# Attention scores by row tiles: one head to 64 rows of the array, keys' low part out of PSUM

## The chip, the cores and the metric

The kernel runs on one core of a Trainium2 chip. The metric is the device time of one execution in microseconds (us). The core's engines run side by side and meet at semaphores: TensorE (PE) multiplies, VectorE (DVE) and ScalarE (ACT) work element by element and are the ones that empty PSUM here, GpSimd (POOL) does arithmetic in SBUF, and SyncE (SP) issues nearly all DMAs.

## The reference, cut to what matters

There are 128 graphs of 128 nodes with 512 features, and one adjacency mask for all. Two layers of attention with 8 heads of 64 follow each other.

```python
def layer0(x, adj, Wq, bq, Wk, bk, Wv, bv, Wo, bo):
    q, k, v = x @ Wq + bq, x @ Wk + bk, x @ Wv + bv        # each split into 8 heads of 64
    scores = einsum('bqhd,bkhd->bhqk', q, k) / sqrt(64) + (1 - adj) * -1e9
    return einsum('bhqk,bkhd->bqhd', softmax(scores), v) @ Wo + bo

x = layernorm(x + layer0(x, adj, ...))
x = layernorm(x + layer1(x, adj, ...))      # the same without Wo and bo
```

## The kernel before, in words

**Tiles.** Two graphs make a group of 256 tokens (`GB = 2`, `T = 256`), 64 groups in all. Products are made in fp32r, a four-byte format of lower precision, and so each operand is split into a high part in fp32r and the low part that is left, and a product is three matmuls: high by high, high by low, low by high. Weights are split once. Queries and keys come out of the projection with features on partitions: tile c of four holds heads 2c (rows 0 to 63) and 2c+1 (rows 64 to 127).

**Scores.** A score matmul needs one head's 64 rows alone. Before, the keys are kept in blocks with zeros: `k_hi[:, b, c]` is 128 x 256, where columns 0 to 127 hold the even head in the upper 64 rows and zeros below, and columns 128 to 255 the odd head in the lower rows and zeros above. One matmul of 128 rows and 256 columns then gives both heads' scores. There are four score banks in PSUM, two to a graph (`ps_score[b][i]`, four heads each).

**Making q and k.** A projection unit (`unit(l, g, u, group, i)`) fills one of two banks, `ps_proj[u % 2]`. Units i = 0, 1 are q, 2 and 3 are k (24 matmuls of 256 columns each), 4 and 5 are v (12 of 512). ScalarE empties q into `q_hi`, VectorE then subtracts (`q_low`, line 848). For k, ScalarE writes the sum with its bias to `k_raw` (line 635), and the bank is free. VectorE casts the two halves of rows into their blocks (line 858) and makes the odd head's low part (line 860), GpSimd makes the even head's (line 1132).

**Order.** Every engine's order is written by hand, as phases A and B of a loop over groups. Phase A of turn g works on scores and softmax of layer 1 of group g-2 and on the projections of layer 0 of group g; phase B on scores of layer 0 of group g and projections of layer 1 of group g-1. On TensorE phase A is: scores, `wo` of the group before, units 0 to 3, attend of graph 0, units 4 and 5, attend of graph 1. Phase B is: scores, units 6 to 10 (i = 0 to 4), attend of graph 0, unit 11 (i = 5), `wo`, attend of graph 1. `need_bank` makes a unit wait until the bank's last user has emptied it; who that is, `emptied` says:

```python
if i < 4:
    return (q_lo_set if i < 2 else k_raw_set)[l], group * 2 + i % 2 + 1
return v_set[l], group * 2 + i - 3
```

**Softmax.** VectorE adds the mask and takes the maximum out of the score banks (line 833), ScalarE takes exponentials (647), VectorE inverts the sums (841), GpSimd scales (1126), VectorE transposes blocks of 32 (893), and DMAs carry them into `prob_t` (302), which attend (451) reads. After attend of layer 0, ScalarE copies to `at_hi` (727), VectorE makes `at_lo` (935) for `wo`; VectorE adds residuals (931, 943), takes statistics (867), GpSimd makes `rstd` (1120) and VectorE normalises (883). GpSimd also adds a bias to a copy of x1 (1138).

Of the kernel before, what the change touches and what calls it, by code (L numbers as in the profile page):

```python
# [16 lines left out]
HALVES = H // HB  # L38
# [17 lines left out]
def adj_resnorm_kernel(nc, x_tok, x_feat, adj, wts, biases, out):  # L56
# [6 lines left out]
    with ExitStack() as ctx:  # L63
# [16 lines left out]
        q_hi, q_lo = sb("q_hi", [P, NC, T], F32R), sb("q_lo", [P, NC, T], F32R)  # L80
        k_hi, k_lo = (sb(n, [P, GB, NC, 2, NODES], F32R) for n in ("k_hi", "k_lo"))
        k_raw = sb("k_raw", [P, 2, T])
# [63 lines left out]
        zeros_set = sem("zeros_set")  # L146
# [9 lines left out]
        k_raw_set = [sem(f"k_raw_set{l}") for l in range(2)]  # L156
        k_hi_set = [sem(f"k_hi_set{l}") for l in range(2)]
        k_lo_even_set = [sem(f"k_lo_even_set{l}") for l in range(2)]
        k_lo_odd_set = [sem(f"k_lo_odd_set{l}") for l in range(2)]
# [68 lines left out]

        def k_block(part, i, e):

            return part[e * HD:(e + 1) * HD, :, 2 * i:2 * i + 2, e, :]

        def k_source(e):
            return k_raw[e * HD:(e + 1) * HD].rearrange("p c (b n) -> p b c n", b=GB)
# [162 lines left out]
        def _(pe):  # L397
# [30 lines left out]
            def scores(l, group, b, banks_free, count):  # L428

                pe.wait_ge(q_lo_set[l], group * 2 + 2)  # L430
                pe.wait_ge(k_lo_even_set[l], group * 2 + 2)
                pe.wait_ge(k_lo_odd_set[l], group * 2 + 2)
                tok = slice(b * NODES, (b + 1) * NODES)
                for i in range(HALVES):

                    need(pe, banks_free, count + 2 * b + i + 1)
                    for c in (2 * i, 2 * i + 1):
                        ps_pair = ps_score[b][i][:, 2 * (c % 2):2 * (c % 2) + 2, :]
                        parts = [(q_hi, k_hi), (q_hi, k_lo), (q_lo, k_hi)]
                        for n, (qp, kp) in enumerate(parts):  # L440
                            last = pe.matmul(ps_pair, qp[:, c, tok], kp[:, b, c], start=(n == 0), stop=(n == 2))  # L441
                    last.then_inc(score_done[l], 1)

            def attend(l, group, b):
# [140 lines left out]
        def _(act):  # L585
# [191 lines left out]
        def _(dve):  # L777
# [167 lines left out]
            def phase_a(g):  # L945
# [40 lines left out]
                if live(g):  # L986
                    k_split(0, g, 0)
# [259 lines left out]
```

## Time and profile before

| | |
|---|---|
| median of three runs | 3415.47 us (3413.94 to 3415.5) |
| span of the profiled execution | 3412.5 us |
| PE busy | 3262.3 us, 96% of the span |
| DVE busy | 2875.9 us, 84% |
| ACT busy | 1697.6 us, 50% |
| POOL busy | 1558.5 us, 46% |
| granted clock of TensorE, mean | 0.991 |

The median lies 3.0 us over the span that the profile covers. Busy time of PE is that of matmuls in a pipeline, so that it covers small waits too; the distance from one matmul's start to the next (its pitch) tells more than its duration.

### The profile page before, as it was taken

Reading aid. Unit: us, or ns where it says so; the run is one execution under the profiler, and the core shown is the slowest. Engines: PE = TensorE matmul, PEld = TensorE weight load, DVE = VectorE, ACT = ScalarE, POOL = GpSimd, SP = SyncE. Lnnn points to the kernel's source line nnn. Section 1 sums busy time; section 2 is a strip of 40 time slices with the busy share of each in tenths; the row PEclk is TensorE's granted clock in tenths of the full one; section 3 lists DMA queues with packets and bytes.
Section 4 is the critical chain, followed back from the end, with each engine's and each line's share of the span. In section 5 each row is a group of like instructions: output and inputs, shape, how many; then the busy total and the mean of one; then the engine's idle time right before and its main releaser. Section 6 shows DMA issues by size and latency. Waiting matters only on the chain.

```text
span 3412.5 us, 78555 instructions
## 1 busy us (share of the span) xinstructions
PE 3262.3 (96%) x24076; PEld 2921.1 (86%) x24076; DVE 2875.9 (84%) x8342; ACT 1697.6 (50%) x5777; POOL 1558.5 (46%) x1350
## 2 busy tenths in 40 slices
PE   6999999999999999999999999999999999999995
PEld 5888888888888888888888888888888888888884
DVE  6888888888888888888888888888888888888885
ACT  4554454455445544544554555455445545554552
POOL 2444444444444444444444444444444444444442
PEclk8999999999999999999999999999999999999997
DMA  4233333333333333333333333333333333333332
GB/s 141 75 95 93 86 90 95 92 86 90 93 92 85 95 94 85 92 92 92 86 91 95 90 83 95 95 84 95 90 92 86 92 95 89 84 95 95 85 93 65
DMA packets 346122, 310.46 MB, mean 91 GB/s; under 512 B 38896, under 2 KB 301296, under 8 KB 346096
## 3 DMA queue, kind: packets, MB, share of 16 engines
q1 hardware_dynamic: 344800, 309.48, 35.0%
q10 hardware_dynamic: 1296, 0.67, 0.1%
q8 instruction: 12, 0.20, 0.0%
q14 instruction: 14, 0.11, 0.0%
HBM read 75.11 MB, written 33.55 MB: 32 GB/s over the span
## 4 chain that ended last, share of the span: by engine, by line
PE 37%; issue 22%; DVE 22%; DMA 5%; POOL 5%; SPq 3%; ACT 3%; DVEq 1%; POOLq 0%; ACTq 0%
PE ps_proj L405 28%; PE ps_score L441 6%; DMA prob_t<-blocks_t 5%; DVE prob L833 4%; DVE k_hi L858 3%; SPq L302 3%; DVE xt_hi L795 3%; ACT k_raw L635 3%; DVE blocks_t L893 2%; PE ps_att L451 2%; DVE x_res L943 2%; POOL k_lo L1132 2%; POOL prob L1126 2%; DVE x L883 2%; PE ps_proj L414 1%
## 5 line engine op out<-in xcount | busy, mean ns | idle before, releaser
L647 ACT ACTIVATE prob<-prob,neg_max 128x128 f32<-128x128 f32 x2048 | 792.6, 390 | 341.5 <-DVE neg_max L833 341.4
L1126 POOL TENSOR_TENSOR prob<-prob,inv_sum 128x512 f32<-128x512 f32 x512 | 523.1, 1043 | 867.1 <-DVE inv_sum L841 867.1
L1132 POOL TENSOR_TENSOR k_lo<-k_raw,k_hi 64x512 fp32r<-64x512 f32 x256 | 388.4, 1517 | 664.9 <-DVE k_hi L858 664.9
L405 PE MATMUL ps_proj<-xt_hi,w_hi_q 128*128 128x256 f32 x2048 | 593.3, 290 | 36.0 <-ACT xt_hi L657 13.5
L405 PE MATMUL ps_proj<-xt_lo,w_hi_q 128*128 128x256 f32 x2048 | 581.4, 284 | 0.0
L405 PE MATMUL ps_proj<-xt_hi,w_lo_q 128*128 128x256 f32 x2048 | 581.2, 284 | 0.0
L405 PE MATMUL ps_proj<-xt_hi,w_hi_k 128*128 128x256 f32 x2048 | 579.8, 283 | 0.8 <-DVE q_lo L848 0.8
L405 PE MATMUL ps_proj<-xt_lo,w_hi_k 128*128 128x256 f32 x2048 | 579.6, 283 | 0.0
L405 PE MATMUL ps_proj<-xt_hi,w_lo_k 128*128 128x256 f32 x2048 | 579.3, 283 | 0.0
L860 DVE TENSOR_TENSOR k_lo<-k_raw,k_hi 64x512 fp32r<-64x512 f32 x256 | 571.2, 2231 | 8.8
L833 DVE CUSTOM_DVE_ANT_0 prob<-ps_score,mask 128x128 f32<-128x128 f32 x2048 | 462.0, 284 | 4.8 <-issue 0.7
L405 PEld LDWEIGHTS ps_proj<-xt_hi,w_hi_q 128*128 128x128 f32 x2048 | 394.3, 193 | 63.5 <-issue 25.4
L635 ACT ACTIVATE k_raw<-ps_proj,bk_col 128x256 f32<-128x256 f32 x512 | 312.8, 719 | 244.2 <-PE ps_proj L405 140.6
L893 DVE STREAM_TRANSPOSE blocks_t<-prob 128x512 f32<-128x512 f32 x512 | 340.7, 694 | 97.9 <-POOL prob L1126 88.3
L414 PE MATMUL ps_proj<-w_hi_v,xt_hi 128*128 128x512 f32 x1024 | 415.0, 405 | 0.3 <-ACT k_raw L635 0.3
L414 PE MATMUL ps_proj<-w_lo_v,xt_hi 128*128 128x512 f32 x1024 | 402.0, 393 | 0.0
L414 PE MATMUL ps_proj<-w_hi_v,xt_lo 128*128 128x512 f32 x1024 | 398.5, 389 | 0.0
L405 PEld LDWEIGHTS ps_proj<-xt_lo,w_hi_q 128*128 128x128 f32 x2048 | 394.9, 193 | 0.1
L405 PEld LDWEIGHTS ps_proj<-xt_hi,w_lo_q 128*128 128x128 f32 x2048 | 394.7, 193 | 0.0
L405 PEld LDWEIGHTS ps_proj<-xt_hi,w_hi_k 128*128 128x128 f32 x2048 | 393.2, 192 | 1.2 <-DVE q_lo L848 1.0
L405 PEld LDWEIGHTS ps_proj<-xt_lo,w_hi_k 128*128 128x128 f32 x2048 | 393.2, 192 | 0.0
L405 PEld LDWEIGHTS ps_proj<-xt_hi,w_lo_k 128*128 128x128 f32 x2048 | 393.2, 192 | 0.0
(89 smaller groups left out, 6928.3 us busy)
## 6 DMA issues: line engine op xcount, KB each, us to landing
prob_t<-blocks_t SPq DMA_DIRECT2D x1024, 128.0 KB, 2.7
y<-x_feat SPq DMA_DIRECT2D x128, 256.0 KB, 2.7
x_res<-x_tok SPq DMA_DIRECT2D x64, 512.0 KB, 3.4
prob_t<-prob SPq DMA_DIRECT2D x512, 64.0 KB, 2.1
out<-y SPq DMA_DIRECT2D x128, 256.0 KB, 2.7
prob_t<-blocks_t SPq DMA_DIRECT2D x256, 64.0 KB, 2.1
y<-y SPq DMA_DIRECT2D x256, 64.0 KB, 2.1
prob<-w_q SPq DMA_DIRECT2D x2, 512.0 KB, 5.8
```

The lines of the kernel that those rows point to most:

```text
L302: sp.dma_start(prob_t[b][:, n].rearrange("p e c q -> p (e c q)"), blocks_t[n * SQ:(n + 1) * SQ].rearrange("p n e c q -> p n (e c q)")).the ...
L405: last = pe.matmul(ps_out[:, i * T:(i + 1) * T], wp[:, c, cols], xp[:, c, :], start=(c == 0 and n == 0), stop=(c == NC - 1 and n == 2))
L414: last = pe.matmul(ps_out[:, :], xp, wp[:, c, :], start=(c == 0 and n == 0), stop=(c == NC - 1 and n == 2))
L441: last = pe.matmul(ps_pair, qp[:, c, tok], kp[:, b, c], start=(n == 0), stop=(n == 2))
L635: last = act.activation(dst, src, ACT.Identity, bias=bias[:, m:m + 1])
L647: last = act.activation(prob[b][:, i, n, :], prob[b][:, i, n, :], ACT.Exp, bias=neg_max[l][b][:, i, n:n + 1], scale=-1.0, accum_out=row_su ...
L795: dve.tensor_copy(x0_half(xt_hi[0], half), x0_half(xt_raw, half)).then_inc(x0_hi_set, 1)
L833: last = dve.tensor_tensor_reduce(prob[b][:, i, n, :], ps_score[b][i][:, n, :], mask[l][:], -SCALE, BIG, ALU.add, ALU.min, neg_max[l][b][: ...
L860: dve.tensor_tensor(k_block(k_lo, i, 1), raw, hi.bitcast(F32), ALU.subtract).then_inc(k_lo_odd_set[l], 1)
L893: dve.transpose(blocks_t[:, :, i].rearrange("p n h q -> p h n q"), prob[b][:, i].rearrange("p h (n k) -> p h n k", k=SQ)).then_inc(blocks_ ...
L1126: pool.tensor_tensor(prob[b][:, i], prob[b][:, i], inv_sum[l][b][:, i, :].unsqueeze(2).to_broadcast([P, HB, NODES]), ALU.mult).then_inc(no ...
L1132: pool.tensor_tensor(k_block(k_lo, i, 0), k_source(0), k_block(k_hi, i, 0).bitcast(F32), ALU.subtract).then_inc(k_lo_even_set[l], 1)
```

## The change

The score matmuls take one head each: 64 rows, the even head on the upper row tile of the array, the odd one on the lower, 128 columns, in turn, and each into a bank of its own (`ps_score[b][e]` now holds the four even or the four odd heads). The keys lose their zero blocks and have the layout of the queries. ScalarE writes `k_hi` straight from the bank, VectorE makes `k_lo` from the bank and `k_hi` as it does for q, in four instructions a unit, with a stride of 32 elements in SBUF. `k_raw`, its casts, GpSimd's share and the clearing of the blocks at the start are gone. Both score banks of a graph are awaited before its first score matmul. A bank of k counts as emptied once `k_lo` is written.

```diff
-        k_hi, k_lo = (sb(n, [P, GB, NC, 2, NODES], F32R) for n in ("k_hi", "k_lo"))
-        k_raw = sb("k_raw", [P, 2, T])
+        k_hi, k_lo = (sb(n, [P, NC, T], F32R) for n in ("k_hi", "k_lo"))
...
-                    return (q_lo_set if i < 2 else k_raw_set)[l], group * 2 + i % 2 + 1
+                    return (q_lo_set if i < 2 else k_lo_set)[l], group * 2 + i % 2 + 1
...
-                for i in range(HALVES):
-
-                    need(pe, banks_free, count + 2 * b + i + 1)
-                    for c in (2 * i, 2 * i + 1):
-                        ps_pair = ps_score[b][i][:, 2 * (c % 2):2 * (c % 2) + 2, :]
-                        parts = [(q_hi, k_hi), (q_hi, k_lo), (q_lo, k_hi)]
-                        for n, (qp, kp) in enumerate(parts):
-                            last = pe.matmul(ps_pair, qp[:, c, tok], kp[:, b, c], start=(n == 0), stop=(n == 2))
-                    last.then_inc(score_done[l], 1)
+                need(pe, banks_free, count + 2 * b + 2)
+                parts = [(q_hi, k_hi), (q_hi, k_lo), (q_lo, k_hi)]
+                for c in range(NC):
+                    for n, (qp, kp) in enumerate(parts):
+                        for e in range(HALVES):
+                            rows = slice(e * HD, (e + 1) * HD)
+                            last = pe.matmul(ps_score[b][e][:, c, :], qp[rows, c, tok], kp[rows, c, tok],
+                                             start=(n == 0), stop=(n == 2))
+                            if c == NC - 1 and n == 2:
+                                last.then_inc(score_done[l], 1)
...
-                        dst = k_raw[:, n, :].rearrange("p (b j n) -> p b n j", b=GB, n=SQ)
+                        dst = k_hi[:, m, :].rearrange("p (b j n) -> p b n j", b=GB, n=SQ)
...
-                for e in range(2):
-                    hi, raw = k_block(k_hi, i, e), k_source(e)
-                    dve.tensor_copy(hi, raw).then_inc(k_hi_set[l], 1)
-                dve.wait_ge(k_hi_set[l], group * 4 + 2 * i + 2)
-                dve.tensor_tensor(k_block(k_lo, i, 1), raw, hi.bitcast(F32), ALU.subtract).then_inc(k_lo_odd_set[l], 1)
+                    for b in range(GB):
+                        tok = slice(b * NODES, (b + 1) * NODES)
+                        hi, lo = (t[:, m, tok].rearrange("p (j n) -> p n j", n=SQ) for t in (k_hi, k_lo))
+                        last = dve.scalar_tensor_tensor(lo, src[:, tok].rearrange("p (n j) -> p n j", j=BLK),
+                                                        bk_col[l][:, m:m + 1], hi.bitcast(F32),
+                                                        ALU.add, ALU.subtract)
+                last.then_inc((q_lo_set if i < 2 else k_lo_set)[l], 1)
...
-                if live(m):
-                    k_low_even(1, m, 1)
                     copy_x1(m, 0)
                     copy_x1(m, 1)
```

TensorE's order around the attend of graph 0 in phase B of turn 2, before; `ps_proj1` is the bank of the second v unit, `w_hi_v1` the weights of layer 1's v:

```order
L414 MATMUL ps_proj0<-w_hi_v1,xt_lo1 128x512
L451 MATMUL ps_att<-prob_t0,v_first 64x128 [waits v_set0,probt_in0,at1_set]
L451 MATMUL ps_att<-prob_t0,v_first 64x128 x7
L414 MATMUL ps_proj1<-w_hi_v1,xt_hi1 128x512 [waits k_raw_set1]
L414 MATMUL ps_proj1<-w_lo_v1,xt_hi1 128x512
```

And the same place now:

```order
L382 MATMUL ps_proj0<-w_hi_v1,xt_lo1 128x512
L419 MATMUL ps_att<-prob_t0,v_first 64x128 [waits v_set0,probt_in0,at1_set]
L419 MATMUL ps_att<-prob_t0,v_first 64x128 x7
L382 MATMUL ps_proj1<-w_hi_v1,xt_hi1 128x512 [waits k_lo_set1]
L382 MATMUL ps_proj1<-w_lo_v1,xt_hi1 128x512
```

The order is the same; the unit's first matmul now waits for the semaphore of VectorE's `k_lo` instead of that of ScalarE's copy.

VectorE's order in the same phase B from the last transposes to the residual, before (`rstd1` and `y` belong to layer 1's layernorm, `at_lo` to the attend of layer 0):

```order
L893 STREAM_TRANSPOSE blocks_t<-prob1 128x4x4x32 [waits norm_set0]
L931 TENSOR_TENSOR y<-prob_t1,x1_res 128x4x4x32 [waits x1_lo_set,y_out1,x1t_in1,x1_res_set,x0_lo_set,at1_in1]
L867 BN_STATS stats1<-y 128x6 [waits sum_set1]
L870 BN_AGGR mean_var1<-stats1 128x2 [waits stats_set1]
L872 TENSOR_SCALAR var_eps1<-mean_var1 128x1 [waits mean_set1]
L935 TENSOR_TENSOR at_lo<-ps_att,at_hi 128x512 [waits at_hi_set]
L883 TENSOR_SCALAR y<-y,mean_var1,rstd1 128x512 [waits rstd_set1]
L858 CAST k_hi<-k_raw 64x2x2x128 [waits k_raw_set1]
L858 CAST k_hi<-k_raw 64x2x2x128
L860 TENSOR_TENSOR k_lo<-k_raw,k_hi 64x2x2x128 [waits k_hi_set1]
L943 TENSOR_TENSOR x_res<-ps_proj0,x_res 128x512 [waits x_res_set,wo_done]
```

And now:

```order
L841 STREAM_TRANSPOSE blocks_t<-prob1 128x4x4x32 [waits norm_set0]
L879 TENSOR_TENSOR y<-prob_t1,x1_res 128x4x4x32 [waits x1_lo_set,y_out1,x1t_in1,x1_res_set,x0_lo_set,at1_in1]
L815 BN_STATS stats1<-y 128x6 [waits sum_set1]
L818 BN_AGGR mean_var1<-stats1 128x2 [waits stats_set1]
L820 TENSOR_SCALAR var_eps1<-mean_var1 128x1 [waits mean_set1]
L883 TENSOR_TENSOR at_lo<-ps_att,at_hi 128x512 [waits at_hi_set]
L831 TENSOR_SCALAR y<-y,mean_var1,rstd1 128x512 [waits rstd_set1]
L805 SCALAR_TENSOR_TENSOR k_lo<-ps_proj1,bk_col1,k_hi 128x32x4 [waits k_hi_set1]
L805 SCALAR_TENSOR_TENSOR k_lo<-ps_proj1,bk_col1,k_hi 128x32x4 x3
L891 TENSOR_TENSOR x_res<-ps_proj0,x_res 128x512 [waits x_res_set,wo_done]
```

The place of k's work is unchanged, behind `at_lo` and the normalise of `y`; four instructions stand for three. (In this unrolled turn there is no group whose x0 is cast between them; in the loop `x0_high` stands ahead of the residual.)

GpSimd in phase B, before:

```order
L1120 TENSOR_TENSOR rstd1<-var_eps1,minus_half 128x1 [waits ln_set1,eps_set1]
L1131 REGISTER_ALU
L1132 TENSOR_TENSOR k_lo<-k_raw,k_hi 64x2x2x128 [waits k_hi_set1]
L1136 REGISTER_ALU
L191 REGISTER_ALU [waits ln_set0]
L1138 TENSOR_TENSOR x1_res<-x1,bv1_row 128x512 [waits sum_set1]
L1138 TENSOR_TENSOR x1_res<-x1,bv1_row 128x512 [waits sum_set1,ln_set0]
```

And now:

```order
L1066 TENSOR_TENSOR rstd1<-var_eps1,minus_half 128x1 [waits ln_set1,eps_set1]
L1077 REGISTER_ALU
L166 REGISTER_ALU [waits ln_set0]
L1079 TENSOR_TENSOR x1_res<-x1,bv1_row 128x512 [waits sum_set1]
L1079 TENSOR_TENSOR x1_res<-x1,bv1_row 128x512 [waits sum_set1,ln_set0]
```

The two copies of x1 have moved up: nothing that waits for keys stands between them and `rstd` now.

## Rows read from the trace of the kernel before

**Rows 1.** The page: span and busy times.
```profile
span 3412.5 us, 78555 instructions
PE 3262.3 (96%) x24076; PEld 2921.1 (86%) x24076; DVE 2875.9 (84%) x8342; ACT 1697.6 (50%) x5777; POOL 1558.5 (46%) x1350
```

**Rows 2.** Windows: one turn of the loop; stretch, length, busy times, clock, DMA.
```profile
1696.87:1748.91 52.04, 50.74 (x378) 45.44 (x377) 44.43 (x131) 26.26 (x90) 24.31 (x21) 1.00 0.35 91
```

**Rows 3.** Waits of the whole run: total us, times, longest.
```profile
PE ps_att L451 <- DMA prob_t<-blocks_t: 66.6, 62, 1.2
PE ps_proj L405 <- DVE x_res L943: 11.6, 61, 0.2
```

**Rows 4.** Timeline, end of phase A: start, length, engine, line, operation, idle before.
```profile
1741.16 0.60 ACT L663 ACTIVATE prob<-ps_att 128x512 f32<-128x512 f32 x1 [2.56 <-PE ps_att L451]
1742.03 1.24 ACT L635 ACTIVATE k_raw<-ps_proj,bk_col 128x256 f32<-128x256 f32 x2 [0.28 <-DVE k_lo L860]
...
1746.43 0.39 PE L414 MATMUL ps_proj<-w_hi_v,xt_lo 128*128 128x512 f32 x1
...
1747.88 0.20 PEld L451 LDWEIGHTS ps_att<-prob_t,v_second 128*64 128x64 f32 x4 [1.49 <-DMA prob_t<-blocks_t]
1747.89 1.09 PE L451 MATMUL ps_att<-prob_t,v_second 128*64 128x128 f32 x16 [1.07 <-DMA prob_t<-blocks_t]
```

**Rows 5.** Timeline of PE around the first attend of phase B.
```profile
1763.28 0.28 PE L405 MATMUL ps_proj<-xt_hi,w_lo_k 128*128 128x256 f32 x1
1763.40 0.40 PE L414 MATMUL ps_proj<-w_hi_v,xt_hi 128*128 128x512 f32 x1
...
1765.92 0.39 PE L414 MATMUL ps_proj<-w_hi_v,xt_lo 128*128 128x512 f32 x1
1766.24 1.09 PE L451 MATMUL ps_att<-prob_t,v_first 128*64 128x128 f32 x16
1767.27 0.50 PE L414 MATMUL ps_proj<-w_hi_v,xt_hi 128*128 128x512 f32 x1
```

**Rows 6.** Groups of weight loads (PEld): busy, mean ns of one.
```profile
L441 PEld LDWEIGHTS ps_score<-k_lo,q_hi 128*128 128x128 f32 x1024 | 195.6, 191 | 0.1
L451 PEld LDWEIGHTS ps_att<-prob_t,v_first 128*64 128x64 f32 x2048 | 110.7, 138 | 55.1 <-issue 46.9
```

**Rows 7.** Timeline of the other engines in phase B.
```profile
1761.97 0.88 DVE L858 CAST k_hi<-k_raw 64x512 fp32r<-64x512 f32 x2 [1.08 <-ACT k_raw L635]
...
1763.13 0.19 ACT L647 ACTIVATION_READ_ACCUMULATOR prob<-prob,neg_max 128x1 f32 x1
...
1764.57 0.24 DVE L841 RECIPROCAL inv_sum<-row_sum 128x4 f32<-128x4 f32 x2
...
1769.37 0.68 DVE L935 TENSOR_TENSOR at_lo<-ps_att,at_hi 128x512 fp32r<-128x512 f32 x1
1769.53 0.55 POOL L1120 TENSOR_TENSOR rstd<-var_eps,minus_half 128x1 f32<-128x1 f32 x1 [2.65 <-DVE var_eps L872]
...
1771.07 1.52 POOL L1132 TENSOR_TENSOR k_lo<-k_raw,k_hi 64x512 fp32r<-64x512 f32 x1 [0.99 <-DVE k_hi L858]
...
1772.55 3.15 POOL L1138 TENSOR_TENSOR x_res<-x,bv_row 128x512 f32<-128x512 f32 x2
1773.17 1.38 DVE L795 CAST xt_hi<-y 128x512 fp32r<-128x512 f32 x1
```

**Rows 8.** Single lines' durations: ns at least, median, at most.
```profile
L848 DVE SCALAR_TENSOR_TENSOR q_lo<-ps_proj,bq_col,q_hi x512: 472/476/485, 18.0 to 3365.6; 128x256 fp32r<-128x256 f32 x171
L833 DVE CUSTOM_DVE_ANT_0 prob<-ps_score,mask x2048: 250/285/294, 38.1 to 3385.1; 128x128 f32<-128x128 f32 x187
...
L635 ACT ACTIVATE q_hi<-ps_proj,bq_col x512: 450/469/483, 16.7 to 3364.7; 128x256 fp32r<-128x256 f32 x171
L635 ACT ACTIVATE k_raw<-ps_proj,bk_col x512: 678/720/747, 24.1 to 3371.8; 128x256 f32<-128x256 f32 x171
...
L883 DVE TENSOR_SCALAR y<-y,mean_var,rstd x128: 516/545/1509, 146.0 to 3409.4; 128x512 f32<-128x512 f32 x128
```

More of the change, by code:

```diff
@@ L37 @@
 HB = 4
-HALVES = H // HB
+HALVES = 2
 NC = D // P
@@ L155, in adj_resnorm_kernel @@
         q_lo_set = [sem(f"q_lo_set{l}") for l in range(2)]
-        k_raw_set = [sem(f"k_raw_set{l}") for l in range(2)]
         k_hi_set = [sem(f"k_hi_set{l}") for l in range(2)]
-        k_lo_even_set = [sem(f"k_lo_even_set{l}") for l in range(2)]
-        k_lo_odd_set = [sem(f"k_lo_odd_set{l}") for l in range(2)]
+        k_lo_set = [sem(f"k_lo_set{l}") for l in range(2)]
         v_done = [sem(f"v_done{l}") for l in range(2)]
@@ L227, in need_bank @@
                     return
[L229 to L234, printed above, removed]
         def x0_half(part, half):
@@ L605, in _, with qk_out @@
             act.wait_ge(small_in, 16 * 9)
-            def zero_k():
-                act.wait_ge(zeros_set, 1)
-                for part in (k_hi, k_lo):
-                    for b in range(GB):
-                        act.activation(part[:, b].rearrange("p c e n -> p (c e n)"), x1[:].rearrange("p b n -> p (b n)"),
-                                       ACT.Copy).then_inc(zeros_set, 1)
-            def qk_out(l, u, group, i, taken_by, times, split_by, halves_split):
-                act.wait_ge(qk_done[l], group * 4 + i + 1)
-                if i < 2:
-                    need(act, score_done[taken_by], times)
-                else:
-                    need(act, k_lo_even_set[split_by], halves_split)
-                    need(act, k_lo_odd_set[split_by], halves_split)
+            def qk_out(l, u, group, i, taken_by, times):
+                act.wait_ge(qk_done[l], group * 4 + i + 1)
+                need(act, score_done[taken_by], times)
                 for n in range(2):
@@ L635, in qk_out @@
                     last = act.activation(dst, src, ACT.Identity, bias=bias[:, m:m + 1])
-                last.then_inc((q_hi_set if i < 2 else k_raw_set)[l], 1)
+                last.then_inc((q_hi_set if i < 2 else k_hi_set)[l], 1)
             def v_out(l, u, group, b, used_by, times):
@@ L673, in q_or_k @@
                         l, last = (1, j) if att else (0, g - 1)
-                        qk_out(0, i, g, i, l, last * 4 + 4,
-                               *((0, g * 2 + 1) if i == 3 else (l, last * 2 + 2)))
+                        qk_out(0, i, g, i, l, last * 4 + 4)
                 def at1_out(b):
@@ L691, in phase_a @@
                 q_or_k(0)
-                if isinstance(g, int) and g == 0:
-                    zero_k()
                 if att:
@@ L719, in q_or_k @@
                         l, last = (0, g) if att else (1, m - 1)
-                        qk_out(1, 6 + i, m, i, l, last * 4 + 4,
-                               *((1, m * 2 + 1) if i == 3 else (l, last * 2 + 2)))
+                        qk_out(1, 6 + i, m, i, l, last * 4 + 4)
                 def at_high(b):
@@ L1128, in normalise_probs @@
                                        ).then_inc(norm_set[l], 1)
-            def k_low_even(l, group, i):
-                pool.wait_ge(k_hi_set[l], group * 4 + 2 * i + 1)
-                pool.tensor_tensor(k_block(k_lo, i, 0), k_source(0), k_block(k_hi, i, 0).bitcast(F32), ALU.subtract
-                                   ).then_inc(k_lo_even_set[l], 1)
             def copy_x1(m, b):
```

64 lines of the change are left out of this document (27 added, 37 removed).

## The prediction

> **What bounds the kernel now.** The page first: TensorE is busy for 96% of the span, VectorE for 84%, GpSimd well under that [rows 1]. The table by windows then gives one turn of the loop, taken from the first score matmul of one phase A to that of the next: 52.04 us, granted clock 1.00 (the upper level, 2.4 GHz), TensorE busy 50.74, VectorE 44.43, GpSimd 24.31 [rows 2]. There are 64 groups, one a turn, so 1 us a turn is 64 us. TensorE is the bound: what is added to its stream, or makes it wait, is added to the time. The table of waits shows how little it waits for now: 66.6 us over the run before attend for the DMAs that bring prob_t, 11.6 us for residual0 to free a projection bank [rows 3]; the reader should note that neither is a wait for a bank of k. In the turn looked at, PE sits idle for 1.07 us before the second attend [rows 4]. A faster VectorE can give back these two and no more: some 1.1 us a turn, and at residual0 0.2 idle and as much again in matmuls that then start afresh.
>
> **The score matmuls.** Before, a turn has 48 of them (128 rows, 256 columns), at the pitch of the projections' [rows 5], 0.12 us: 5.76 us. After, 96 of 64 rows and 128 columns, as 48 pairs on two row tiles. No row has such a pair. From below: 512 columns take 0.229 us (11 pitches from 1763.40 to 1765.92), 256 take 0.12, so 128 more or fewer columns are 0.054 us, and a pair that truly runs as one would take 0.067 us. From above: the weight load of 128 columns takes 0.191 us and that of 64 columns 0.138 [rows 6]; the difference says 0.107 us for 128 columns as they stream in, so two loads one behind the other, with 0.013 us that 256 columns take over their streaming, are 0.227 us a pair. Between them: attend works with two column tiles already; its 16 records (eight fp32 matmuls, two passes each, weight loads of 64 columns) take 1.03 us from 1766.24 to 1767.27, 0.129 us for two [rows 5], which two loads of 64 columns in turn (0.107) would explain too. But at 1747.88 four such loads are through in 0.20 us [rows 4]; in turn they would need 0.138 + 3 x 0.053 = 0.30, so loads into different column tiles do go side by side. I take the loads of the two tiles as side by side, one pair for each 0.107 us load, and some overhead, nearer to attend's pair than to either end: 0.115 us, 5.5 us a turn, a gain of 0.25. The array changes its tiling where scores end, twice a turn more than now; at attend such a change costs 0.09 us (1765.92 to 1766.24 is 0.32, not 0.23) [rows 5]: +0.2.
>
> What keeps a pair from 0.067 us by these rows is its loads: each score matmul needs one of 128 columns, 0.107 us. One rule of the Trainium skill is weighed against that. TensorE: Matmul & The Clock Gate, section "Measured speedup vs the span model", says that matmuls on different tiles take the time of one and some 4 ns for each further tile. By it a pair would be 0.058 us, the scores 2.8 us a turn, and the sum below 170 us less. Its cases have 512 columns, and no row here shows a pair of row tiles.
>
> **The low part of the keys.** Removed per k unit on VectorE: two casts and a subtraction, which hold it from 1761.97 to the next instruction at 1764.57, 2.6 us; on GpSimd one subtraction of 1.52 [rows 7]. Added: four additions-and-subtractions of 128 x 128 out of PSUM. The 128x256 form of the same instruction takes 0.476 us (and its longest is 0.485, so GpSimd does not slow it), another 128x128 instruction out of PSUM 0.285 [rows 8]. In between lies 0.34; instructions in a row overlap by 0.08 (two reciprocals of 0.16 in 0.24) [rows 7], so the four take 3 x 0.26 + 0.34 = 1.12 us. Bounds: 0.90 at 0.285 each, and 1.68 if the stride of 32 elements in k_hi and k_lo costs what ScalarE's strided write shows (0.720 against 0.469) [rows 8] and one takes 0.476. VectorE gets 1.5 us a unit back, 6 us a turn. That removes the 1.1 us wait for prob_t (its transposes stand right behind phase A's first k unit, where those 1.5 us go) and the 0.4 at residual0: -1.5 a turn.
>
> **The wait that is added.** A projection bank of k is now free when VectorE has written k_lo, not when ScalarE has copied it: the v unit two units later waits for k_lo_set. The order of VectorE was not changed for it. In phase B the second v unit follows the first attend; the last k unit's VectorE work stands behind at_lo (which needs that same attend, and ScalarE's copy after it) and behind the normalise of y. I follow it in the times of before, with PE ready for the unit at 1767.27 [rows 5, 7]:
> - The earlier k unit is 1.5 us shorter, so the reciprocals start when the exponentials end, 1763.13 + 0.19, 1.2 us before their 1764.57. GpSimd's prob, the transposes, y, statistics and at_lo all move by 1.2: at_lo from 1769.37 to 1768.17 (at_hi is there by then: ScalarE's copy of an attend takes 0.60 us from 0.12 after its end [rows 4]), done at 1768.85.
> - rstd moves from 1769.53 to 1768.33, done at 1768.88. The normalise may then start.
> - But GpSimd's next instruction is no longer the low part of k, which waited until 1771.07; it is the copy of x1, ready, two in a row of about 1.5 us. Where a cast of VectorE meets such a copy now, the cast (1773.17) takes 1.38 us and ends 0.4 us after half of the two copies' 3.15. The normalise is of the kind that shows this too: 0.545 at the median, 1.509 at most [rows 7, 8]. So it ends at 1768.87 + 1.48 + 0.45 = 1770.8.
> - Four instructions, 1.12: 1771.9. PE is held for 4.6 us; I take 4.5.
> Without that collision the normalise ends at 1769.4 and PE is held 3.2 us: the lower bound. If it loses against both copies, 6.0.
> Behind it on TensorE stand unit 5 of layer 1, wo, the second attend and all scores of phase A, so nothing of it is hidden: x0_high, wo and residual0 all come later by as much.
> In phase A the same wait falls on the second v unit: ScalarE's copy of attend ends at 1741.76, its k unit (1.24) at 1743.0, VectorE's four at 1744.15; PE gets there 11 pitches of 0.228 ahead of the unit's last matmul at 1746.43, at 1743.93 [rows 4]: +0.25, up to 0.8 with slow strides. The wait for both score banks costs nothing: their masks are through some 20 us before.
>
> **The sum per turn:** 4.5 + 0.25 + 0.2 - 0.25 - 1.5 = +3.2 us, 64 turns 205 us. 3412.5 + 205 + 3.0 (the median of the runs stands 3.0 over the profiled span) = 3620 us.
>
> **The rivals.**
> - The two row tiles load or stream one behind the other: 48 pairs at 0.22 to 0.24 us instead of 0.115, +5.0 to +6.0 a turn, 3940 to 4005 us. For it: attend's pair takes no less than its two loads in turn. Against: the four loads in 0.20 us; but those are column tiles. 22%.
> - The pairs run as one, at 0.067 us: scores 3.2 us, -2.3 a turn, 3475 us. For it: 256 columns hide a load of 128 at 0.12 us, and whether the load bounds them can't be read. Against: 0.107 us a load. 9%. The page named above says the same of such a pair.
> - Faster than before: that, and GpSimd not in the way of the normalise (3.2 for 4.5): +3.2 - 2.3 - 1.3 = -0.4 a turn, 3390. It decides when the hold of PE is under 3.6 us with pairs under 0.07. 3%; and 1% for a time within 0.2%.
> - Within the forecast's case (65%): strides slow (+0.56 in phase B and as much in phase A, +70 us) and the normalise behind both copies (+1.5, +95 us) raise it to 3790; a hold of 3.2 lowers it to 3535.
> - That the chain that I build does not bind, because VectorE reaches the last k unit before at_lo, is excluded by its order.
>
> **How the numbers follow.** Likeliest 3620. The forecast's own case spans 3535 to 3790; the range 3530 to 3950 reaches over it to the edge of the serial pairs and leaves out the fast ones (12%) and the slower half of the serial ones. What a measurement of this kernel can tell from no change is about 0.2%. Faster 0.03, same 0.01, slower 0.96.
>
> **What would show it.** In the waits: PE ps_proj waiting for DVE k_lo, 64 times and some 4.5 us each, around 290 us in all, and next to nothing left of the waits for prob_t and x_res; y's second normalise near 2 us in the loop; k_lo 0.34 each; scores from first to last matmul 2.8 us a phase. Wrong if scores take 1.6 or 5.5 us a phase, or if that wait is missing: then VectorE was somewhere else than I think.

## The result and the profile after

The changed kernel takes 3783.18 us, the median of 4 runs (3780.33 to 3785.0), against 3415.48 for the kernel before (3413.94 to 3416.75): a ratio of 1.1077, interval 1.1062 to 1.1093. It is 11% slower. The prediction said 3620, with a range of 3530 to 3950. The sign, the place and, by errors that nearly cancel, the size of the added wait were right; a term of 2.8 us a turn was missing.

The page of the changed kernel's profile, its span and busy times (for the kernel before: [rows 1]):
```profile
span 3781.5 us, 84318 instructions
PE 3427.0 (91%) x27148; PEld 3031.9 (80%) x27148; DVE 2511.1 (66%) x8598; ACT 1692.6 (45%) x5773; POOL 1148.0 (30%) x1093
```
TensorE's share falls from 96 to 91%, and still its busy time grows by 165 us. Both need a reason: idle time alone gives the first, but not the second. The waits of PE over the run [rows 3]:
```profile
PE ps_proj L382 <- DVE k_lo L805: 289.1, 127, 4.2
```
The waits for prob_t and for x_res are gone, as foretold, and the new one is there. The table by windows, first one turn (52.04 us and clock 1.00 in [rows 2]; both windows run from phase B's scores to the next phase B's scores, not from phase A's as the prediction says, and no term of the sum hangs on that), then three pieces of it in phase B: from the first attend to the start of the second v unit, then 5.71 us, then the rest up to the second attend. Columns: length, busy PE, PEld, VectorE, ScalarE, GpSimd, then the granted clock, DMA share and GB/s.
```profile
1759.57:1817.59 58.02, 53.42 (x426) 47.31 (x424) 39.19 (x134) 26.22 (x90) 17.92 (x17) 0.94 0.32 81
1777.12:1782.44 5.32, 1.09 (x17) 0.85 (x17) 5.10 (x11) 1.09 (x2) 3.19 (x3) 0.91 0.54 136
1782.44:1788.15 5.71, 5.71 (x13) 4.51 (x14) 0.27 (x1) 0.18 (x1) 1.27 (x1) 0.50 0.21 67
1788.15:1790.86 2.71, 2.71 (x12) 1.96 (x10) 0.00 (x0) 0.41 (x1) 0.00 (x0) 0.97 0.00 0
```
The third row is the surprise. PE is busy all the time, and the granted clock is 0.50: the lower of the two levels, 1.2 GHz. Only 13 matmuls start in its 5.71 us; the fourth row has about as many in 2.71. The timeline of the same place (start, length, engine, line, operation, idle before):
```profile
1777.12 1.09 PE L419 MATMUL ps_att<-prob_t,v_first 128*64 128x128 f32 x16
...
1778.26 0.60 ACT L677 ACTIVATE at_hi<-ps_att 128x512 fp32r<-128x512 f32 x1 [2.83 <-PE ps_att L419]
...
1778.89 0.69 DVE L883 TENSOR_TENSOR at_lo<-ps_att,at_hi 128x512 fp32r<-128x512 f32 x1
1778.96 0.55 POOL L1066 TENSOR_TENSOR rstd<-var_eps,minus_half 128x1 f32<-128x1 f32 x1 [2.65 <-DVE var_eps L820]
1779.48 2.67 POOL L1079 TENSOR_TENSOR x_res<-x,bv_row 128x512 f32<-128x512 f32 x2
1779.55 1.48 DVE L831 TENSOR_SCALAR y<-y,mean_var,rstd 128x512 f32<-128x512 f32 x1
1780.95 1.44 DVE L805 SCALAR_TENSOR_TENSOR k_lo<-ps_proj,bk_col,k_hi 128x128 fp32r<-128x128 f32 x4
...
1782.44 0.80 PE L382 MATMUL ps_proj<-w_hi_v,xt_hi 128*128 128x512 f32 x1 [4.23 <-DVE k_lo L805]
...
1783.03 0.63 PE L382 MATMUL ps_proj<-w_lo_v,xt_hi 128*128 128x512 f32 x1
...
1783.46 0.63 PE L382 MATMUL ps_proj<-w_hi_v,xt_lo 128*128 128x512 f32 x1
...
1788.46 0.40 PE L382 MATMUL ps_proj<-w_hi_o,at_lo 128*128 128x512 f32 x1
...
1788.70 0.40 PE L382 MATMUL ps_proj<-w_hi_o,at_hi 128*128 128x512 f32 x1
```
Read it downward. The chain of VectorE is the predicted one: at_lo, the normalise of y (1.48 us beside GpSimd's two copies of x1, the first of which starts 0.07 us before it), the four k_lo (1.44), and only then the v unit, after 4.23 us of idle time. After that the 512-column matmuls come every 0.43 us (1783.03 to 1783.46), and from 1788.46 on every 0.23 to 0.24, as in [rows 5]. The single lines (ns at least, median, at most; [rows 8]):
```profile
L805 DVE SCALAR_TENSOR_TENSOR k_lo<-ps_proj,bk_col,k_hi x1024: 415/450/473, 24.2 to 3743.4; 128x128 fp32r<-128x128 f32 x171
L831 DVE TENSOR_SCALAR y<-y,mean_var,rstd x128: 515/547/1495, 147.2 to 3778.5; 128x512 f32<-128x512 f32 x128
L589 ACT ACTIVATE k_hi<-ps_proj,bk_col x512: 662/714/752, 22.8 to 3741.6; 128x256 fp32r<-128x256 f32 x171
```

### The profile page after: what moved, and what is told of

Same layout as the page of the kernel before. It is cut to its first block, busy times and chain, and to the rows that moved or that the text cites. A ratio compares the mean times of both kernels' runs of the same rounds, so it can differ in the third digit from the quotient of the medians.

```text
span 3781.5 us, 84318 instructions
## 1 busy us (share of the span) xinstructions
PE 3427.0 (91%) x27148; PEld 3031.9 (80%) x27148; DVE 2511.1 (66%) x8598; ACT 1692.6 (45%) x5773; POOL 1148.0 (30%) x1093
## 4 chain that ended last, share of the span: by engine, by line
issue 47%; PE 27%; POOL 14%; DVE 10%; ACT 1%; POOLq 1%; DVEq 0%; DMA 0%; SPq 0%; ACTq 0%
PE ps_proj L382 17%; POOL prob L1072 8%; PE ps_proj L373 7%; POOL x_res L1095 3%; DVE k_lo L805 3%; PE ps_score L407 2%; DVE stats L815 2%; POOL xt_lo L1058 1%; POOL rstd L1066 1%; DVE at_lo L883 1%; PE ps_att L419 1%; DVE y L879 1%; DVE x_res L891 1%; DVE mean_var L818 1%; DVE var_eps L820 0%
## 5 line engine op out<-in xcount | busy, mean ns | idle before, releaser
L382 PE MATMUL ps_proj<-w_hi_v,xt_hi 128*128 128x512 f32 x1024 | 492.7, 481 | 289.1 <-DVE k_lo L805 289.1
L382 PEld LDWEIGHTS ps_proj<-w_hi_v,xt_hi 128*128 128x128 f32 x1024 | 225.1, 220 | 399.0 <-DVE k_lo L805 344.2
L805 DVE SCALAR_TENSOR_TENSOR k_lo<-ps_proj,bk_col,k_hi 128x128 fp32r<-128x128 f32 x1024 | 385.8, 445 | 163.8 <-ACT k_hi L589 163.8
L382 PE MATMUL ps_proj<-w_lo_v,xt_hi 128*128 128x512 f32 x1024 | 461.5, 451 | 0.0
L382 PE MATMUL ps_proj<-w_hi_v,xt_lo 128*128 128x512 f32 x1024 | 459.8, 449 | 0.0
L891 DVE TENSOR_TENSOR x_res<-ps_proj,x_res 128x512 f32<-128x512 f32 x128 | 88.1, 688 | 525.1 <-PE ps_proj L382 525.1
L373 PEld LDWEIGHTS ps_proj<-xt_hi,w_hi_q 128*128 128x128 f32 x2048 | 394.1, 192 | 32.7 <-ACT xt_hi L611 14.1
L595 ACT ACTIVATE v_second<-ps_proj 128x512 f32<-128x512 f32 x128 | 76.4, 597 | 717.3 <-PE ps_proj L382 717.3
```

The costliest lines, as they stand in the source:

```text
L373: last = pe.matmul(ps_out[:, i * T:(i + 1) * T], wp[:, c, cols], xp[:, c, :], start=(c == 0 and n == 0), stop=(c == NC - 1 and n == 2))
L382: last = pe.matmul(ps_out[:, :], xp, wp[:, c, :], start=(c == 0 and n == 0), stop=(c == NC - 1 and n == 2))
L595: act.activation(v[l][b][:], ps_proj[u % 2][:, :], ACT.Copy).then_inc(v_set[l], 1)
L805: last = dve.scalar_tensor_tensor(lo, src[:, tok].rearrange("p (n j) -> p n j", j=BLK), bk_col[l][:, m:m + 1], hi.bitcast(F32), ALU.add, A ...
L891: dve.tensor_tensor(x_res[:, b, :], ps_proj[b][:, :], x_res[:, b, :], ALU.add).then_inc(sum_set[0], 1)
```

## The experiments

All ran beside the kernel before, whose medians there were 3414.6 to 3414.8 us. Line numbers in fences are those of each kernel.

**1. The last k unit of phase B earlier on VectorE.** The same work in another order: its k_lo ahead of the transposes of attention 1, so no longer behind at_lo and the normalise.
```diff
@@ VectorE, phase B
+                if live(m):
+                    qk_low(1, 9, m, 3)
                 if att:
                     transpose_blocks(0, g, 1, probt_in[0], g * per + per // 2)
@@ later, ahead of x0_high
-                if live(m):
-                    qk_low(1, 9, m, 3)
                 if not isinstance(g, int) or g + 1 < G:
                     x0_high(g + 1, 0)
```


> The changed kernel with VectorE's last k unit of phase B (k_lo of the second k unit, layer 1) moved ahead of the transposes of graph 1, so that it no longer stands behind at_lo and the normalise. Theory A (the hold of the second v unit for k_lo costs 4.3 us a turn, and the half clock that follows it costs 2.6 more, both from that hold alone): hold and half clock both gone, turn 58.0 - 6.9 = 51.1 us, time 3340 to 3370. Theory B (the clock falls because score matmuls use half the rows): the hold goes, the clock stays at 0.94, time about 3515. Theory C (VectorE as a whole is late because of slow strided k_lo): another wait takes the place, 3700 or more.

Measured: 3345.02 us, ratio 0.9797 (0.9780 to 0.9813). The granted clock over the run is 0.992 instead of 0.936. The waits:
```profile
PE ps_proj L382 <- DVE k_lo L805: 24.8, 64, 0.6
```
What stays is phase A's wait. The hold of phase B and all that follows from it are worth 438 us, 6.8 a turn, of which 4.3 are idle time. So the changed kernel with one block moved is about 2% faster than the kernel before. The edit to the scores and keys is not what costs; the place of k_lo in VectorE's order is.

**2. The hold filled with matmuls.** Are the missing 2.8 us due to the clock, or to something else behind the hold? Between the first attend and the v unit come 16 matmuls of 512 columns whose results nobody reads (work added, into a score bank whose scores have been taken).
```diff
                     attend(0, g, 0)
+                    if proj:
+                        pe.wait_ge(masked_set[0], g * 4 + 4)
+                        for n in range(16):
+                            pe.matmul(ps_score[0][0][:].rearrange("p h n -> p (h n)"), xt_hi[1][:, n % NC, :NODES],
+                                      w_hi["v1"][:, n % NC, :], start=True, stop=True)
                 layer1_unit(5)
```


> The changed kernel with 16 extra matmuls of 512 columns, whose results nothing uses, on TensorE where it waits for k_lo in phase B (about 3.7 us of work in a hold of 4.3). Theory A: the hold's end stays where it is, but the v unit behind it runs at the full clock: 2.6 us a turn less, about 3620. Theory B: the clock still falls, 3780 or more.

Measured: 3619.64 us, ratio 1.0601 (1.0583 to 1.0618), clock 0.992. Timeline of PE:
```profile
1758.31 1.09 PE L419 MATMUL ps_att<-prob_t,v_first 128*64 128x128 f32 x16
1759.33 3.92 PE L508 MATMUL ps_score<-w_hi_v,xt_hi 128*128 128x512 f32 x16
1763.71 0.50 PE L382 MATMUL ps_proj<-w_hi_v,xt_hi 128*128 128x512 f32 x1 [0.46 <-DVE k_lo L810]
1764.04 0.39 PE L382 MATMUL ps_proj<-w_lo_v,xt_hi 128*128 128x512 f32 x1
1764.27 0.40 PE L382 MATMUL ps_proj<-w_hi_v,xt_lo 128*128 128x512 f32 x1
```
The v unit starts as late as before (5.4 us after attend's start), yet its matmuls come every 0.23 us. More work on TensorE, and 163.5 us less time: that is the price of the lower clock, 2.6 us a turn, and 3619.64 is what the changed kernel takes without it. The prediction's 3620 was that number, though not each of its terms (below).

**3. GpSimd's copies of x1 behind its low part of x0.** This takes them away from the normalise, the collision that the prediction priced at 1.3 us a turn.
```diff
@@ GpSimd, phase B
-                if live(m):
-                    copy_x1(m, 0)
-                    copy_x1(m, 1)
                 if live(g):
                     if not isinstance(g, int) or g + 1 < G:
                         x0_low(g + 1, 0)
+                if live(m):
+                    copy_x1(m, 0)
+                    copy_x1(m, 1)
```


> The changed kernel with GpSimd's two copies of x1 moved behind its x0_low, so that the normalise of y meets no GpSimd work. The prediction's term for that collision was 1.3 us of the hold: hold 3.3 instead of 4.3, normalise 0.55 instead of 1.48 us. With the clock falling as now: about 3715. If the shorter hold keeps the clock up, 2.6 us a turn less again: 3550. If the collision isn't what delays k_lo: 3780.

Measured: 3661.51 us, ratio 1.0722 (1.0704 to 1.0740), clock 0.956. The normalise takes 0.55 us, and from attend's start to the v unit it is 4.39 us instead of 5.33, so 0.94 of hold is gone. Of the 122 us gained about 60 are hold; the rest comes from the 24 matmuls behind it, which take 7.36 us in the mean of all turns instead of 8.39. Neither number that was expected is met, because the turns differ: with the same 3.3 us of idle time the clock doesn't fall at all in 10 turns (5.7 us for the 24 matmuls), and elsewhere they take 7.1 to 8.5 us.

**4. The kernel before with the added wait alone.** Scores and keys as before, without row tiles, but a bank of k counts as free only when VectorE's k_lo (the odd heads' part) is written. Is the lower clock something that the row tiles bring?
```diff
-                    return (q_lo_set if i < 2 else k_raw_set)[l], group * 2 + i % 2 + 1
+                    return (q_lo_set if i < 2 else k_lo_odd_set)[l], group * 2 + i % 2 + 1
```


> The kernel before, its scores and its k work untouched, with one change: a projection bank of k counts as emptied when VectorE's k_lo (odd heads) is written, so TensorE's v units wait for it. Theory A: in before's times k_lo of phase B ends at 1773.1 and TensorE is ready at 1767.3, so a hold of 5.8 us, and a half clock behind it of 2.6; less 1.4 us of waits that vanish: some 7 us a turn more than before, 3850. Theory B (half clock from row tiles): no half clock, 3680.

Measured: 4219.8 us, ratio 1.2358 (1.2338 to 1.2379), clock 0.917; much more than expected.
```profile
PE ps_proj L414 <- DVE k_lo L860: 637.3, 254, 4.5
```
By windows, in phase A the long wait with the 12 matmuls ahead of it and then the 12 behind it; and in phase B the 24 behind its wait:
```profile
1760.34:1767.01 6.67, 3.02 (x13) 2.18 (x13) 6.57 (x7) 2.25 (x4) 3.80 (x2) 1.00 0.51 130
1767.01:1771.55 4.54, 4.54 (x13) 3.27 (x13) 0.67 (x1) 0.00 (x0) 0.00 (x0) 0.62 0.11 26
1796.82:1804.91 8.09, 8.09 (x25) 6.20 (x25) 1.36 (x1) 0.60 (x1) 3.73 (x3) 0.68 0.11 34
```
With VectorE's old, long work on k all four v units of a turn wait, 254 waits and 10.0 us a turn, and a low clock follows the long wait in phase A (0.62 in the second row) and that in phase B (0.68 in the third). No row tile is in this kernel: the idle time brings the clock down. It also shows what the shorter work on k is worth where banks hang on it: with the wait the kernel is 805 us slower than before, and the changed kernel, which has it too, 368.

**5. The kernel before with row-tile scores alone.** Compact k_hi and k_lo made from k_raw as before, the scores as in the change, no zero blocks. The edit of the scores:
```diff
-                            last = pe.matmul(ps_pair, qp[:, c, tok], kp[:, b, c], start=(n == 0), stop=(n == 2))
+                        for e in range(HALVES):
+                            rows = slice(e * HD, (e + 1) * HD)
+                            last = pe.matmul(ps_score[b][e][:, c, :], qp[rows, c, tok], kp[rows, b, c],
+                                             start=(n == 0), stop=(n == 2))
```


> The kernel before with the score matmuls alone changed: 64 rows and 128 columns on two row tiles, compact k_hi and k_lo, still made from k_raw by VectorE and GpSimd in their old shares, banks of k free after k_raw. Theory A: scores 2.83 us a phase instead of 2.97, one more change of tiling (0.09) a phase, so within 0.1 us a turn of before: 3405 to 3420, clock 0.99. Theory B (row tiles bring the clock down): clock under 0.97, 3500 or more.

Measured: 3412.6 us, ratio 0.9994 (0.9985 to 1.0003), clock 0.991. The row tiles by themselves do nothing that can be measured here: in the turn looked at, its two phases take 2.83 and 2.99 us of scores where 2.97 stood twice, and TensorE still waits for prob_t, 68.6 us in all.

**6. The three products of a head in a row,** the even tile's three, then the odd tile's three, instead of one from each.
```diff
-                    for n, (qp, kp) in enumerate(parts):
-                        for e in range(HALVES):
+                    for e in range(HALVES):
+                        for n, (qp, kp) in enumerate(parts):
```


> The changed kernel with each head's three products in a row, then the other head's three, instead of alternating between the row tiles. If a pair costs 0.112 us because the two tiles' weight loads run side by side, and a load of 128 columns takes 0.107: three in a row on one tile take 0.107 each, scores 10 to 11 us a turn instead of 5.66, time 4050 to 4120 (if TensorE reorders nothing), or less where the loads of the other tile are pulled ahead. If the tiles are independent of order: unchanged, 3783.

Measured: 3781.99 us, ratio 1.1075 (1.1055 to 1.1096). No change. Timeline of PE in the scores:
```profile
1791.25 0.28 PE L407 MATMUL ps_score<-k_lo,q_hi 64*128 64x128 f32 x2
1791.36 0.28 PE L407 MATMUL ps_score<-k_hi,q_lo 64*128 64x128 f32 x2
1791.48 0.28 PE L407 MATMUL ps_score<-k_hi,q_hi 64*128 64x128 f32 x2
```
Each row holds two matmuls, and there is one row for each 0.11 us. It can mean two things: that matmuls of the two tiles run together even from this order, or that each takes 0.056 us by itself, one behind the other, with no gain from tiles. Runs 9 and 10 were made to tell these apart. The single records of this run speak for the first: two starts are 0.01 us apart, the next 0.10 behind.

**7. Contiguous keys.** k_hi and k_lo are written contiguously in SBUF; the stride (of 4) moves to the PSUM operand.
```diff
-                        hi, lo = (t[:, m, tok].rearrange("p (j n) -> p n j", n=SQ) for t in (k_hi, k_lo))
-                        last = dve.scalar_tensor_tensor(lo, src[:, tok].rearrange("p (n j) -> p n j", j=BLK),
+                        hi, lo = (t[:, m, tok].rearrange("p (j n) -> p j n", n=SQ) for t in (k_hi, k_lo))
+                        last = dve.scalar_tensor_tensor(lo, src[:, tok].rearrange("p (n j) -> p j n", j=BLK),
@@ ScalarE: the same for dst and src of k_hi
```


> The changed kernel with k_hi and k_lo written in rows of 32 contiguous elements, the stride (4 elements) now on the read side in PSUM, on ScalarE and VectorE. If it is the stride of 32 elements in SBUF that makes k_lo 0.45 us (0.34 was predicted): 0.34 each, ScalarE's k_hi 0.47 instead of 0.72, 0.4 to 0.5 us less of hold in phase B and 0.5 less in phase A: about 3725. If strides cost the same in PSUM: no change, 3783.

Measured: 3613.16 us, ratio 1.0582 (1.0566 to 1.0598), clock 0.957.
```profile
L805 DVE SCALAR_TENSOR_TENSOR k_lo<-ps_proj,bk_col,k_hi x1024: 333/341/353, 24.8 to 3572.6; 128x128 fp32r<-128x128 f32 x171
L589 ACT ACTIVATE k_hi<-ps_proj,bk_col x512: 466/472/482, 23.4 to 3571.3; 128x256 fp32r<-128x256 f32 x171
```
k_lo takes the 0.34 us of the prediction, so the rest of its 0.45 was the stride. ScalarE's k_hi falls from 0.71 to 0.47. Phase A's wait is gone (64 waits for k_lo are left, 212.9 us). In phase B the hold is 0.84 us shorter, and k_lo is less than half of that:
```profile
1756.19 1.02 DVE L831 TENSOR_SCALAR y<-y,mean_var,rstd 128x512 f32<-128x512 f32 x1
1757.13 1.11 DVE L805 SCALAR_TENSOR_TENSOR k_lo<-ps_proj,bk_col,k_hi 128x128 fp32r<-128x128 f32 x4
```
The normalise takes 1.02 us instead of 1.48. In both kernels it ends 0.28 us after GpSimd's first copy of x1, and here it starts 0.53 us after that copy's start instead of 0.07. The time gained, 170 us, is more than the waits lost (76 us): the 24 matmuls behind the hold take 7.48 us in the mean of all turns (7.03 in the one looked at) instead of 8.39.

**8. Both phases earlier.** Run 1, and in phase A ScalarE's last k_hi ahead of its copy of attend's result and VectorE's last k_lo ahead of the transposes.
```diff
@@ ScalarE, phase A
-                at1_out(0)
                 q_or_k(3)
+                at1_out(0)
@@ VectorE, phase A
-                if live(j):
-                    transpose_at1(j, 0)
                 if live(g):
                     qk_low(0, 3, g, 3)
+                if live(j):
+                    transpose_at1(j, 0)
```


> e1 with phase A mended too: ScalarE empties the second k unit of layer 0 before it copies attend's result, and VectorE makes its k_lo before it transposes that result. Theory A: neither v unit waits for k_lo, turn about 50.8 us, 3310 to 3340, faster than before by 2 to 3%. If something else of the same length takes the place of the wait in phase A (transposes of attend's result come 1.5 us later): as e1.

Measured: 3301.54 us, ratio 0.9667 (0.9654 to 0.9681), a little under what was expected; of the waits for k_lo 0.8 us are left.

**9. The kernel before with each score matmul split in two.** The head's 128 columns and the 128 of zeros apart: 96 matmuls a turn, on all 128 rows, the same data.
```diff
-                        for n, (qp, kp) in enumerate(parts):
-                            last = pe.matmul(ps_pair, qp[:, c, tok], kp[:, b, c], start=(n == 0), stop=(n == 2))
+                        for e in range(2):
+                            for n, (qp, kp) in enumerate(parts):
+                                last = pe.matmul(ps_pair[:, e, :], qp[:, c, tok], kp[:, b, c, e], start=(n == 0), stop=(n == 2))
```


> The kernel before, with each score matmul of 256 columns (head's columns and zeros) split into two of 128 columns: 96 of 128 rows and 128 columns a turn instead of 48 of 256, no row tiles, the same waits and the same work elsewhere. Theory A (what the run with the tiles' products in turn suggests: a matmul of 128 columns takes 0.056 us by its own columns, and its weight load never limits it, so the row tiles do nothing for the rate): each phase's scores take 2.7 to 2.9 us, the time is that of the kernel before, 3405 to 3425. Theory B (what the prediction held: each matmul needs a weight load of 128 columns, 0.107 us, and only loads into two different row tiles go side by side): 96 x 0.107 to 0.12 = 10.3 to 11.5 us of scores a turn instead of 5.9, about 5 us a turn more, 3700 to 3780.

Measured: 3694.4 us, ratio 1.0822 (1.0805 to 1.0838), clock 0.992. Timeline of PE:
```profile
1810.50 0.28 PE L442 MATMUL ps_score<-k_lo,q_hi 128*128 128x128 f32 x1
1810.61 0.28 PE L442 MATMUL ps_score<-k_hi,q_lo 128*128 128x128 f32 x1
1810.73 0.27 PE L442 MATMUL ps_score<-k_hi,q_hi 128*128 128x128 f32 x1
1810.84 0.27 PE L442 MATMUL ps_score<-k_lo,q_hi 128*128 128x128 f32 x1
```
One matmul for each 0.11 us, though its columns are half of those of [rows 5]: 5.41 us of scores a phase instead of 2.97. Theory B holds, a little under its 3700. A matmul of 128 columns that has the array alone gets no cheaper than 0.11 us, twice the 0.054 that its columns need by [rows 5]; that is also near the 0.107 us which the prediction estimated for its weight load.

**10. One row tile after the other.** All 12 matmuls of the even tile, then the 12 of the odd one.
```diff
-                for c in range(NC):
-                    for n, (qp, kp) in enumerate(parts):
-                        for e in range(HALVES):
+                for e in range(HALVES):
+                    for c in range(NC):
+                        for n, (qp, kp) in enumerate(parts):
```


> The changed kernel with all 12 score matmuls of the even heads' row tile first and then the 12 of the odd heads' tile, instead of one of each in turn. Theory A (a matmul of 128 columns takes 0.056 us of its own, tiles never stream at the same time): 2.8 us of scores a phase as in the changed kernel, 3775 to 3790. Theory B (the pair of tiles overlaps in some way, in loads or in streaming): the scores grow to 4 us or more a phase, 3900 or more.

Measured: 4065.83 us, ratio 1.1907 (1.1885 to 1.1929), clock 0.914. Timeline of PE around a change of tile:
```profile
1803.62 0.27 PE L407 MATMUL ps_score<-k_lo,q_hi 64*128 64x128 f32 x1
1803.72 0.27 PE L407 MATMUL ps_score<-k_hi,q_lo 64*128 64x128 f32 x1
1803.73 0.38 PE L407 MATMUL ps_score<-k_hi,q_hi 64*128 64x128 f32 x2
1803.90 0.32 PE L407 MATMUL ps_score<-k_lo,q_hi 64*128 64x128 f32 x2
1804.01 0.33 PE L407 MATMUL ps_score<-k_hi,q_lo 64*128 64x128 f32 x2
1804.12 0.27 PE L407 MATMUL ps_score<-k_hi,q_hi 64*128 64x128 f32 x1
```
And a piece of the scores of a phase B:
```profile
1770.33 0.27 PE L407 MATMUL ps_score<-k_hi,q_hi 64*128 64x128 f32 x1
1770.44 0.27 PE L407 MATMUL ps_score<-k_lo,q_hi 64*128 64x128 f32 x1
1770.56 0.37 PE L407 MATMUL ps_score<-k_hi,q_lo 64*128 64x128 f32 x1
1770.72 0.42 PE L407 MATMUL ps_score<-k_hi,q_hi 64*128 64x128 f32 x1
1770.94 0.41 PE L407 MATMUL ps_score<-k_lo,q_hi 64*128 64x128 f32 x1
```
Within a tile there is one matmul for each 0.11 us; only where the tile changes do records come in twos, some three pairs at each change. So two tiles do work at the same time, and a lone one doesn't get under 0.111 us a matmul. At full clock a phase's scores take 4.34 us instead of 2.83, 3.0 us a turn. The other 1.4, the remainder, go with the clock: in the second piece TensorE never stops, and still from 1770.56 on its records grow from 0.27 to 0.41 us and the matmuls come every 0.21 us. The clock is below full in 43 of the run's 128 stretches of scores, against one in the changed kernel.

**11. Runs 7 and 8 together.**

> The changed kernel with the last k unit's parts taken earlier in both phases (as the run with both moved) and with k_hi and k_lo contiguous in SBUF, the stride in the PSUM operand instead. The strided k writes cost ScalarE 8 x 0.25 us and VectorE 16 x 0.1 us a turn, off the path once no v unit waits for them. Theory A (PE is the bound once the waits are gone): little more, 3285 to 3303, no wait of ps_proj for k_lo. Theory B (VectorE and ScalarE still end waits of PE): up to 1.5 us a turn more, 3210 to 3280.

Measured: 3282.25 us, the median of 5 runs, ratio 0.9613 (0.9599 to 0.9626): 3.9% faster than the kernel before and 13% faster than the changed one. One turn by windows:
```profile
1779.92:1829.94 50.02, 50.02 (x427) 45.28 (x425) 37.10 (x134) 25.07 (x90) 17.99 (x17) 1.00 0.35 94
```
What is left of two waits:
```profile
PE ps_att L419 <- DMA prob_t<-blocks_t: 0.4, 1, 0.4
...
PE ps_proj L382 <- DVE k_lo L805: 0.2, 1, 0.2
```
PE is busy for all of the 50.02 us. That is theory A, a little under its 3285; what more is to be had must come from fewer or shorter matmuls.

## Why the prediction was right, and what it left out

Run 11 gives a turn without any wait, so each term can be read as a difference of stretches of PE, in us of one turn:

| term of the sum | predicted | measured | from |
|---|---|---|---|
| hold of the second v unit, phase B | +4.5 | +4.3 | attend's start to v unit 5.33, of which attend has 1.02 |
| wait in phase A | +0.25 | +0.67 | the two v units 6.38, in run 11 5.71 |
| scores and changes of tiling | -0.05 | -0.28 | 2 x 2.83 for 2 x 2.97 |
| waits removed | -1.5 | -1.74 | 52.04 - 50.02, less the scores |
| clock behind the hold | none | +2.76 | v unit and wo 8.42, in run 11 5.66 |
| q, k and v units, small gaps | none | +0.27 | 11.77 for 11.61, 2.95 for 2.84 |
| sum | +3.2 | +5.98 | 58.02 - 52.04 |

**The hold** was right in its chain: at_lo, the normalise, four k_lo, in that order, with GpSimd's copies in the way. Its errors nearly cancel. at_lo followed ScalarE's at_hi at once, and so the normalise started 0.2 us sooner after attend than I had it. It took 1.48 us and ended 0.28 us after the first of the two copies, where I had let it take 1.93. The four k_lo took 1.44 instead of 1.12. Run 3 confirms the collision: without it the hold is 0.94 us shorter (priced at 1.3). The total of 289.1 us of waiting, foretold as some 290, is luck in part too: the 63 waits of phase B make 265 of it, and phase A's the other 24.

**The low part of the keys** at 0.34 us was mis-sized: it takes 0.45, near the bound of 0.476 for slow strides that I had named and not taken. Run 7 shows that the stride in SBUF is the reason. The same is why phase A waits longer than I said; in run 7 it doesn't wait.

**The scores** were right, 2.83 us a phase for 2.8, and the reason, which run 6 had put in doubt, stands: one matmul of 128 columns takes 0.111 us by itself (run 9), not the 0.054 of its columns, and two tiles go side by side, a pair in 0.112. That it is the weight load which sets the 0.111 fits the estimate of 0.107, but no run varied the load, so this part is argued and not shown. That the tiles run one behind the other (22%) was wrong, and so was the pair at 0.067 us (9%). The Trainium skill (TensorE: Matmul & The Clock Gate, section "Measured speedup vs the span model") says that matmuls on different tiles take the time of one and a few ns more. The traces agree, 0.112 against 0.111; my reading of it, 0.058 a pair, went wrong in the "time of one", which here is the 0.111 that one takes and not the time of its columns.

**What failed** is "the sum per turn", which lacks a term: it prices the hold at its idle time and lets TensorE go on at the pace of [rows 5]. Behind 4.2 us of idle time it goes on at 1.2 GHz for 5.7 us. Run 2 measures the term alone: 163.5 us, which is all of the 163 us by which the time exceeds 3620. The other terms were off by 0.2 to 0.4 us a turn each (-0.2, +0.4, -0.2, -0.2, +0.3) and cancel, so that 3620 fits run 2 so closely is luck. So is it that 3783 lies inside the range: its upper part was there for serial row tiles, and the 3790 of the forecast's own case for slow strides and a longer collision, which the runs don't bear out in that size. No part of it was there for the clock. The Trainium skill (TensorE: Matmul & The Clock Gate, section "The HAM clock gate") says that TensorE runs at either 1.2 or 2.4 GHz and falls to the lower one after idle time. The rows agree, with a pitch of 0.43 against 0.23 us. A rival of its own, a hold of 4.5 us that is followed by a stretch at the lower clock, belonged in the prediction: [rows 2] shows clock 1.00 in a kernel whose longest waits in a turn were 1.2 us [rows 3], so nothing there said that the pace would hold through four.

Two of my expectations behind the prediction went the same way. In runs 3 and 7 I had taken the slow stretch as fixed. In the mean of all turns it is shorter after a shorter hold (8.39 us of v unit and wo after 4.2 us of idle time, 7.36 after 3.3, 7.48 after 3.4, against 5.67 with none), but turns with the same idle time differ by up to 2.8 us, so that the length of the pause alone doesn't set it. In run 4 I had expected waits in phase B and found them at all four v units.

## What to carry to other kernels

When a bank is freed by another engine than before, find that engine's instruction in its own order and read what stands ahead of it; the edit here was 11% slower or 2% faster than the kernel before, according to where one block of four instructions stood, and 4% faster with phase A's order and the stride mended too. Price a long idle stretch of TensorE at more than its length: look at the granted clock of the stretch behind it. Splitting a matmul to skip zeros broke even here when the pieces went to different tiles in an order that mixed them (run 5), and cost 8% when each had the whole array (run 9): halving the columns from 256 to 128 took a matmul from 0.12 us only to 0.11.

## What the runs showed of the hardware that was not expected

- After 4.2 us without a matmul the granted clock was 0.50 for 5.7 us of unbroken work, 13 matmuls of 512 columns at 0.43 us each, though before the pause it had been at full pace. The cost, 2.6 to 2.8 us, is two thirds of the pause itself. After pauses of 3.3 us (run 3) the clock fell in 51 turns of 61 and not in the other 10.
- The clock can fall without a pause: in run 10, where TensorE's longest idle time in the 20 us before was 0.4 us, with one row tile of 64 rows at work at a time, it fell in the middle of a phase's scores, and the 96 matmuls behind took 14.1 us instead of 11.8. In run 9, with the same pace but all 128 rows, the mean over the run stayed at 0.992. Whether the rows in use are what matters was not tried further.
- Matmuls of two row tiles pair up even when the program has three of one tile in a row (run 6), but not when it has twelve (run 10), where three pairs form at each change of tile.
- fp32r matmuls of 128 columns, each with its own weight load of 128 columns, start every 0.111 us one behind the other, on all 128 rows (run 9) as on one tile of 64 (run 10), while those of 256 columns start every 0.12. The load is the likely pace; no run varied it.
- A stride of 32 elements in SBUF costs VectorE's 128x128 instruction 0.45 us instead of 0.34, and ScalarE's 128x256 one 0.71 instead of 0.47. Those lower times were measured with a stride of 4 in the PSUM operand instead. For ScalarE that costs nothing, since q_hi without any stride takes 0.469; for VectorE no unstrided instruction of this size was measured.
